# Two heads in one output block, half masks, and a new order in the first two attentions of a two-layer decoder

## The reference

```
# first attention: 16 heads of 8 features, causal
q = concat(rms_norm(q_c), q_r);  k = concat(rms_norm(k_c), k_r)
attn = softmax(q @ k.T * scale + triu(-inf));  x = x + (attn @ v) @ W_O.T

# local attention on ctx_1024: chunks of w = 64 positions, so C = 2 chunks;
# each query sees the previous, own and next chunk; a missing chunk gives zero keys and values
ck = stack(prev, own, next);  probs = softmax(q . k_e over 3 * w)
x = x + (probs . v_e) @ Wc

# relative attention of the second layer
score = ((q + u) @ k.T + shift((q + v) @ pos.T)) / sqrt(8)
x = x + softmax(score) @ val @ Wo + bo
```

## Time and profile before

| | us |
|---|---|
| median of 3 runs | 1391.49 (1387.20 to 1395.02) |
| the profiled execution | 1387.54, its span 1385.7 |
| busy: PE, DVE, ACT, POOL | 1139.1, 990.6, 835.2, 562.5 |
| mean granted clock of TensorE | 0.953 |

### The profile page before, as it was taken

How to read it: one execution, slowest core, us unless ns; L and a number is a source line. 1 busy time by engine, 2 the same in 40 slices (tenths; PEclk the granted TensorE clock), 3 DMA queues, 4 the chain that set the end, 5 groups by cost and what they waited for, 6 DMA issues and landing times. The chain is left out here.

```text
span 1385.7 us, 40959 instructions
## 1 busy us (share of the span) xinstructions
PE 1139.1 (82%) x12567; PEld 744.3 (54%) x12567; DVE 990.6 (71%) x3667; ACT 835.2 (60%) x1653; POOL 562.5 (41%) x750
## 2 busy tenths in 40 slices
PE   2788887887598888898589878888888758999998
PEld 1344444454355555555378456666666544665665
DVE  2588888885366666666466369999998739887885
ACT  1487878786277777777423378888887432342331
POOL 4777777772222222222010146666665911111120
PEclk9899999999599999999889999999999778999999
DMA  8000000000100000000022078888887540000000
GB/s 220 9 2 1 0 0 0 0 2 2 56 8 2 1 0 0 0 0 0 17 60 61 14 214 237 236 232 232 234 234 210 155 130 1 8 16 9 8 8 16
DMA packets 170484, 91.33 MB, mean 66 GB/s; under 512 B 8922, under 2 KB 168804, under 8 KB 170132
## 3 DMA queue, kind: packets, MB, share of 16 engines
q1 hardware_dynamic: 169860, 88.05, 23.3%
q0 software_dynamic: 528, 2.10, 0.5%
HBM read 52.11 MB, written 38.01 MB: 65 GB/s over the span
## 5 line engine op out<-in xcount | busy, mean ns | idle before, releaser
L821 POOL TENSOR_TENSOR rr<-ms_eps,minus_half 128x16 f32<-128x16 f32 x64 | 185.2, 2912 | 11.6 <-DVE ms_eps L1029 11.6
L550 PE MATMUL psum<-identb,stacks 128*128 128x128 bf16 x1800 | 138.3, 224 | 34.9 <-DVE stacks L1078 13.5
L1163 DVE TENSOR_REDUCE rowmax<-psum 128x4 f32<-128x768 f32 x128 | 123.1, 961 | 60.8 <-PE psum L2130 60.8
L550 PEld LDWEIGHTS psum<-identb,stacks 128*128 128x128 bf16 x1800 | 111.5, 100 | 65.7 <-issue 24.8
L1364 DVE CUSTOM_DVE_ANT_0 summed<-psum,pos_score 128x128 f32<-128x128 f32 x512 | 117.9, 285 | 23.5 <-PE psum L2330 19.9
L1930 ACT ACTIVATE pos_rows<-psum 128x512 f32<-128x512 f32 x72 | 43.0, 597 | 144.0 <-PE psum L2514 137.1
L2372 PE MATMUL psum<-consts,summed 128*128 128x128 f32 x512 | 84.4, 289 | 43.1 <-DVE summed L1370 41.7
L1068 DVE TENSOR_REDUCE rowmax<-psum 128x4 f32<-128x512 f32 x128 | 84.9, 686 | 34.6 <-PE psum L1996 34.6
L1816 ACT ACTIVATE probsT<-psum 128x512 f32<-128x512 f32 x128 | 76.9, 601 | 54.0 <-PE psum L641 39.8
L641 PE MATMUL psum<-probsT,values 128*32 128x128 f32 x2048 | 85.2, 282 | 26.1 <-DVE attn L667 21.7
L882 POOL TENSOR_TENSOR rest<-staged,stacks 128x128 f32<-128x128 f32 x32 | 13.7, 428 | 220.4 <-ACT stacks L533 220.4
(11 more groups left out here) (320 smaller groups left out, 3065.1 us busy)
## 6 DMA issues: line engine op xcount, KB each, us to landing
skew<-pos_rows SPq DMA_DIRECT2D x128, 258.0 KB, 3.8
pos_score<-skew SPq DMA_DIRECT2D x128, 256.0 KB, 4.0
X<-in_x_dram POOLq DMA_DIRECT2D x1, 2048.0 KB, 12.1
ctxT<-in_ctx_dram SPq DMA_DIRECT2D x1, 2048.0 KB, 10.6
yT<-in_ctx_dram SPq DMA_DIRECT2D x32, 64.0 KB, 1.8
ctxT<-in_ctx_dram SPq DMA_DIRECT2D x32, 64.0 KB, 1.8
out_dram<-X SPq DMA_DIRECT2D x8, 256.0 KB, 2.3
pos_rows<-in_ctx_dram SPq DMA_DIRECT2D x25, 64.0 KB, 1.9
```

What stands on the lines that cost most here:

```text
L550: last = pe.transpose(turned[:, t, :], stacks[:, which, 2 * t:2 * t + 2, :].rearrange("s h k -> s (h k)"), identb[:, :])
L821: pool.tensor_tensor(out=rr[:, par, i * H:(i + 1) * H], in0=ms_eps[:, i * H:(i + 1) * H], in1=minus_half[:, 0:H], op=ALU.pow).then_inc(A.r ...
L1163: dve.tensor_reduce(rowmax[:, par, PT * r:PT * r + PT].rearrange("s (h b) -> s b h", b=2), B.max_space, AX.X, ALU.max, negate=True).then_i ...
```

## The change

It has four parts.

- Output blocks: two heads share one block of 32 rows, the even group in rows 0 to 8, the odd one in rows 16 to 24; the odd group's products accumulate onto the even one's (whose weights are zero there). So `out_bank` is read over 256 columns, `outT` is half as wide, `turn_out` is two transposes and `normalise` one multiplication. Values are written to two places by parity (`value_slots`), and `v8` has a fourth slice.
- Half masks: a mask is four products of 256 columns, each over 64 of the 128 rows, alternating between the two halves of the rows and the two banks. Both banks wait for both maxima (or exponentials).
- Order in the first attention. DVE: `ln_stats` in front of the first `largest`, `query_parts` between the two. ACT: `save_xnT` between the two first parts; `save_again` (the copy of the turned stack with the maxima) behind `exps_turned` 2 and 3. PE: `scores` of the next batch ahead of `scores_turned`.
- Local attention: the two products of `sums` go; DVE adds the two chunks' keys (`key_sums`, from `k3T`), behind `normalise`; `save_kv` copies 128 columns and goes ahead of `save_q`; `key_top_1` and `turn_v` wait for the sums; `ln_stats` goes behind `largest` 2.

The diff, cut:

```diff
-        outT = sb("outT", [128, R, S])
+        outT = sb("outT", [128, R // 2, S])
+        by_pairs = values[:, :, :, :].rearrange("s a (m e) g -> s a m (e g)", e=2).rearrange("s a m (x w) -> s a m x w", w=HD)
+        SLOT_STEP = (GW + GW // 2) // HD
+        def value_slots(i):
+            return by_pairs[:, i, :, 0:SLOT_STEP + 1:SLOT_STEP, :]
...
+        def out_rows(q, r, p):
+            return q.out_bank[p * GW:(p + 1) * GW, (r // 2) * S:(r // 2 + 1) * S]
...
-                last = pe.matmul(q.out_bank[p * GW:(p + 1) * GW, r * S:(r + 1) * S], v, probsT[:, r % 2, p, :],
-                                 start=True, stop=True)
+                last = pe.matmul(out_rows(q, r, p), v, probsT[:, r % 2, p, :], start=(r % 2 == 0), stop=(r % 2 == 1),
+                                 skip_group_check=True)
...
-            act.activation(outT[:, :, :].rearrange("k r s -> k (r s)"), q.out_bank, ACT.Copy).then_inc(q.oT, 1)
+            act.activation(outT[:, :, :].rearrange("k r s -> k (r s)"), q.out_bank[:, 0:R // 2 * S], ACT.Copy).then_inc(q.oT, 1)
...
-            for r in range(R):
-                last = pe.transpose(q.out_bank[:, r * S:(r + 1) * S], outT[:, r, :], ident)
+            for j in range(R // 2):
+                last = pe.transpose(q.out_bank[:, j * S:(j + 1) * S], outT[:, j, :], ident)
...
-            if q.stacked:
-                for half in range(2):
-                    last = dve.tensor_tensor(
...
+            def mask_products(banks, turned):
+                for half in range(2):
+                    for k in range(2):
+                        rows = slice(k * STACK, (k + 1) * STACK)
+                        columns = banks[k].rearrange("s (p k) -> s p k", p=PT)[:, :, half * STACK:(half + 1) * STACK]
+                        pe.matmul(columns, mask_half[turned][rows, half, :], identb[rows, rows].unsqueeze(1).broadcast_to([STACK, PT, STACK]),
+                                  start=(half == 0), stop=False, skip_group_check=True)
             def masks(n, r):
-                for k in range(2):
-                    wait(pe, A.mx, n * R + r + k - 1)
-                    pe.matmul(A.max_bank[k], identb[:, :], causal4[:, :, :].rearrange("s p k -> s (p k)"),
-                              start=True, stop=False, skip_group_check=True)
+                wait(pe, A.mx, n * R + r)
+                mask_products(A.max_bank, 0)
...
+                if left >= 6:
+                    ln_stats(dve, A, b + 6, b + 6)
                 if left >= 2:
                     largest(b + 2, par, 0)
+                if left >= 3:
+                    query_parts(b + 3, 1 - par)
+                if left >= 2:
                     largest(b + 2, par, 1)
                 if left >= 3:
-                    query_parts(b + 3, 1 - par)
                     key_parts(b + 3)
-                if left >= 6:
-                    ln_stats(dve, A, b + 6, b + 6)
...
-                if left >= 1:
-                    save_again(b + 1, 1 - par)
                 if left >= 3:
                     top_query(b + 3, 1 - par)
-                    top_key(b + 3)
                 if left >= 5:
                     save_xnT(act, A, b + 5, xnT[:, :], A.proj, b + 5)
+                if left >= 3:
+                    top_key(b + 3)
                 exps_turned(b, 2)
                 exps_turned(b, 3)
+                if left >= 1:
+                    save_again(b + 1, 1 - par)
...
-                scores_turned(b, par, four, 2)
                 if left >= 2:
                     scores(b + 2, par, after_four, 0)
+                scores_turned(b, par, four, 2)
...
+                def key_sums(n, par):
+                    wait(dve, B.kv, 2 * n + 1)
+                    first, second = [k3T[:, par, c * 64:(c + 1) * 64].unsqueeze(1).broadcast_to([128, 2, 64]) for c in range(2)]
+                    dve.scalar_tensor_tensor(out=k3T[:, par, BOTH:2 * BOTH].rearrange("s (c k) -> s c k", c=2), in0=first,
+                                             scalar=one_rows[:, 0:1], in1=second, op0=ALU.subtract, op1=ALU.add).then_inc(B.kv, 1)
...
+                    if left >= 2:
+                        key_sums(b + 2, par)
+                    if left >= 1:
+                        largest(b + 1, 1 - par, 2)
                     if left >= 3:
                         ln_stats(dve, B, b + 3, b + 3)
-                    if left >= 1:
-                        largest(b + 1, 1 - par, 2)
...
                     if left >= 2:
+                        save_kv(b + 2, par)
                         save_q(b + 2, par)
-                        save_kv(b + 2, par)
...
-                    sums = B.ln_bank[:, 384:512].rearrange("s (c k) -> s c k", c=2)
-                    for c in range(2):
-                        last = pe.matmul(sums, both, ctxT[:, at(n), c * 64:(c + 1) * 64].broadcast_to([D, 2, 64]),
-                                         start=(c == 0), stop=(c == 1))
-                    last.then_inc(B.proj, 1)
```

More of the change, by code:

```diff
@@ L28 @@
 MAX_SLOT = 56
+MASKED = -1e30
 C_ID, C_CAUSAL, C_HEAD, C_REP, C_SIN = 0, 128, 256, 272, 400
@@ L221, in decoder @@
         projected = yT[:, 0:16, :].rearrange("s (a w) (h d) -> s a w h d", a=4, h=H)
-        causalT4 = yT[:, 16:18, :].rearrange("s a k -> s (a k)").bitcast(BF16).rearrange("s (p k) -> s p k", p=PT)
+        causalb = yT[:, 16:17, :].rearrange("s a k -> s (a k)").bitcast(BF16)[:, 0:S]
+        mask_blocks = causal4[:, :, :].rearrange("s (t h) (x w) -> s t (h x) w", t=2, w=S // 2)
+        mask_half = [causal4[:, 2 * turned:2 * turned + 2, :] for turned in range(2)]
         keysT = seqT[:, 0:16, :].rearrange("k a s -> k (a s)").bitcast(BF16).rearrange("k (a t s) -> k a t s", a=4, t=H // 2)
@@ L803, in _ @@
             pool.wait_ge(k0.ones, 1)
-            pool.memset(values[:, :, :, HD:HD + 1], 1.0).then_inc(k0.ones, 1)
+            for half in range(2):
+                ones_at = half * GW // 2 + HD
+                last = pool.memset(values[:, :, half:H:2, ones_at:ones_at + 1], 1.0)
+            last.then_inc(k0.ones, 1)
             pool.memset(minus_half[:, :], -0.5).then_inc(k0.half, 1)
@@ L808, in _ @@
             pool.wait_ge(k0.kvzero, 2)
-            pool.memset(v8[:, :, 0, HD:HD + 1], 1.0).then_inc(k0.kvzero, 1)
             for half in range(2):
+                ones_at = half * GW // 2 + HD
+                last = pool.memset(v8[:, :, half, ones_at:ones_at + 1], 1.0)
+            last.then_inc(k0.kvzero, 1)
+            for half in range(2):
+                ones_at = half * GW // 2 + HD
                 pool.wait_ge(k0.kvzero, 3 + half)
-                pool.memset(v8[half * STACK:(half + 1) * STACK, :, 1 + half, HD:HD + 1], 1.0).then_inc(k0.kvzero, 1)
+                pool.memset(v8[half * STACK:(half + 1) * STACK, :, 2 + half, ones_at:ones_at + 1], 1.0).then_inc(k0.kvzero, 1)
             pool.wait_ge(k0.kvzero, 5)
@@ L1002, in _ @@
             dve.tensor_copy(identb[:, :], ident).then_inc(k0.cast, 1)
-            dve.tensor_copy(causal4[:, :, :], consts[:, C_CAUSAL:C_CAUSAL + S].unsqueeze(1).broadcast_to([S, PT, S])).then_inc(k0.cast, 1)
+            dve.tensor_copy(causalb, consts[:, C_CAUSAL:C_CAUSAL + S]).then_inc(k0.cast, 1)
+            for turned in range(2):
+                dve.memset(mask_blocks[:, turned, 1 + turned, :], 0.0)
+                dve.memset(mask_blocks[:, turned, 2 - turned, :], MASKED)
             dve.wait_ge(k0.mask, 1)
-            dve.tensor_copy(causalT4[:, :, :], A.key_bank.bitcast(BF16)[:, 0:S].unsqueeze(1).broadcast_to([S, PT, S])).then_inc(k0.mask, 1)
+            for half in range(2):
+                rows = slice(half * STACK, (half + 1) * STACK)
+                keys_first = A.key_bank.bitcast(BF16)[rows, half * STACK:(half + 1) * STACK]
+                queries_first = consts[rows, C_CAUSAL + half * STACK:C_CAUSAL + (half + 1) * STACK]
+                for turned, triangle in enumerate([keys_first, queries_first]):
+                    last = dve.tensor_copy(mask_blocks[rows, turned, 0:4:3, :], triangle.unsqueeze(1).broadcast_to([STACK, 2, STACK]))
+            last.then_inc(k0.mask, 1)
             dve.tensor_scalar(qnws[:, :], qnw[:, :], SCALE, None, ALU.mult).then_inc(k0.qnws, 1)
@@ L1211, in cross_attention @@
                     ln_apply(dve, B, n, n)
+                    key_sums(n, n)
                     key_rest_of(n, n)
@@ L1687, in save_v @@
                     wait(act, B.o, (n - 3) * R)
-                    act.activation(v8[:, four, 0, 0:HD], B.ln_bank[:, USED:USED + HD], ACT.Copy)
+                    both = v8[:, four, 0:2, :].rearrange("s e g -> s (e g)").rearrange("s (x w) -> s x w", w=HD)[:, 0:SLOT_STEP + 1:SLOT_STEP, :]
+                    act.activation(both, B.ln_bank[:, USED:USED + HD].unsqueeze(1).broadcast_to([S, 2, HD]), ACT.Copy)
                     for half in range(2):
                         rows = slice(half * STACK, (half + 1) * STACK)
```

(5 more changed lines are left out.)

56 lines of the change are left out of this document (24 added, 32 removed).

## The result

The changed kernel takes 1339.76 us (median of 4 runs, 1338.67 to 1345.12), the kernel before, in runs beside it, 1390.43: a ratio of 0.964, 95% interval 0.960 to 0.968. The forecast was 1347, faster. The profiled execution is one of 1338.67, its span 1336.9 (before 1385.7).

What follows compares the result with a forecast made beforehand. Rings of waits bound the first and local attention, VectorE the relative one. Gains of 30+9+2+1.5=42.5 us from 1387.5 gave 1345, plus half of the 4 us to the run median: 1347; 8-in-10 range 1325 to 1368.

Steps and rivals of the forecast that it cites:

- DVE's own work: 8.15-0.07=8.08: First attention: with PE no longer waited for, a batch is VectorE's own work, 8.08 us, taken as 8.1 instead of 9.13.
- 1.74 instead of 1.96: First attention: upper end of the gain, 36 us, if the six operations on parts take 1.74 us instead of 1.96.
- First rival, a new wait there: First attention: waits among three nearly full engines make the batch 8.5 us, gain 18 instead of 30, total 1359; chance 0.2.
- The cover of 1.90 us: First attention: VectorE has 1.27 plus 0.63 = 1.90 us of work while TensorE does its piece, 0.43 to spare.
- PE's piece: First attention: TensorE's products from `turn_again` to the scores, forecast at 1.47 us after the change, 2.25 before including the semaphore.
- the ring itself: Local attention: waits over query copy, GpSimd's parts, `place_max`, `save_again`, `save_outT` and `project` set the 9.55 us batch; gain 0.3.
- it was about 0.2 us from being the later one: Local attention: the second path, exponential of the sums, value products, `turn_again`, caps the gain, about 0.2 us from being later.
- 9.55-0.29=9.26: Local attention: net 0.29 us less on the ring, from halved `save_outT`, no wait for `project`, less 0.17 for `save_kv` first.
- the local attention gains nothing: Rival: copying keys ahead of queries and the second path eat the local gain; 9 us less, 1356; chance 0.12.
- DVE, the bound, only `normalise`: Relative attention: VectorE, busy 260.8 of 292 us, is the bound; only `normalise` shortens, 32 times 0.07 = 2 us.
- The 1.5 us for the ends: Ends of the three attentions: `outT`, `turn_out` and `normalise` each save 0.21+0.25+0.07=0.53 us, 1.5 in all.
- The clock rival: First attention: an idler TensorE falls to half clock, its 6.6 us a batch becoming 11.1; kernel slower, up to 1435; chance 0.03.

## Why the prediction was right, and where it was not

**First attention: mechanism right, size too small.** The idle time in front of `largest` 0, the half masks side by side (0.45 against the 0.44 forecast for two groups) and DVE's own work as the new bound are there. The term that was mis-sized is "DVE's own work: 8.15-0.07=8.08". It measured 7.77. Of the 0.31, 0.33 is the query parts (1.18 to 0.85): 0.21 as GpSimd's addition no longer meets the conversion but a reduction from PSUM, which it doesn't stretch (0.68), and 0.12 as an independent reduction follows the third operation. Another 0.08 is a slip in the reckoning: the 8.15 counted `key_3` to its recorded end (231.28), but with work behind it the next operation starts 0.21 after its start, not 0.29. Against these stand 0.07 for the statistics (0.63 before, 0.70 now) and 0.03 for the key parts. The text had the faster parts as an end of its range ("1.74 instead of 1.96": they measured 0.85+0.89=1.74, and by the distance of starts they had taken 1.18+0.86=2.04 before) and did not take it. The runs with late parts and with the cut residual show both causes. Masks and statistics put back together cost 0.73 a batch and the parts 0.32, of the 1.36 that went (9.13 to 7.77); the new order of the scores and of ACT's copies and the halved output were not undone by themselves, so how the rest divides is open.

**First rival, a new wait there: not so.** The wait of the mask for two maxima costs PE 0.35 us and DVE nothing. The cover of 1.90 us was right (172.44 to 174.33: 1.89), while PE's piece is 1.60 (late statistics), not 1.47: 0.29 to spare, not 0.43. With full masks it is 2.02 (229.67 to 231.69, with both edits), where 1.90 was forecast.

**Local attention: the step that failed** is the ring itself, and with it "it was about 0.2 us from being the later one" (and even with 0.2 in hand, 0.3 a batch could not come). The text followed the batch over the query copy, `project` and GpSimd's parts to `place_max`, and saw the path over the exponential of the sums and the value products as the second. That second path already set the pace in the kernel before: there `turn_again` follows 0.15 behind the end of `place_max`, where 0.06 is enough if nothing else holds it (230.01 to 230.07), and it starts 0.35 behind the start of the value products, in both kernels. The ring that it closes had the same 9.05 us apart from `normalise` before and after. What the text priced did come true, on a path that does not bind: from `save_again` to the end of the next `place_max` it is 8.42 instead of 8.75, 0.33 less where 0.29 was forecast, and `turn_again` now follows that end by 0.42 instead of 0.15. With `turn_again` early the value products are out of the way and it follows `place_max` again; the batch then falls to 9.27 to 9.32, near the 9.55-0.29=9.26 of the text, but other waits bind there too, so that nearness proves nothing. What shortens only the earlier of two near equal paths gains nothing. The rival "the local attention gains nothing" was nearly the true case, though for one only of its two reasons, the second path: of the 2.3 us within the stage the batches explain 2.0 (31 times 0.063), and the run with two multiplications puts these down to `normalise`, 0.06 a batch, a term that the text had in the other two attentions and not in this ring. The other reason, the copy of the keys ahead of the queries, was not it: turning the two round changed nothing.

**Relative attention: the step "DVE, the bound, only `normalise`" failed, and the size is luck.** Its period fell by 0.009 (9.034 to 9.025), not by 0.07: in both kernels the next operation on DVE starts 0.38 or 0.48 behind the multiplication's start, in turn (0.48 at 937.42 to 937.90 before, 0.38 at 882.10 to 882.48 after), and later in the batch DVE idles as before (0.45, and 0.46 after), by its bracket for PE. "DVE, the bound" was read from a busy share of 89%; the batch was set elsewhere. The run with two multiplications there confirms that the merged one is worth nothing. Which wait sets this batch stays open. One candidate that the text did not weigh is the DMA traffic of this stage, 223 GB/s at a busy share of 0.83 before and 224 at 0.83 after (the earlier trace rows and above); no run separates it from a wait. Of the stage's 2.1 us the periods explain 0.3 (31 times 0.009). The others are within what the stage differs by from trace to trace.

**Stage ends and clock.** The 1.5 us for the ends can't be told apart from what else happens there: 1.8 went between the first two stages and 1.0 in the rest, 0.6 came between the second and third, and 2.2 went ahead of the first reciprocal, which the sum did not have at all. The clock rival did not come: granted clock 0.99 in the first attention with PE busy 192.97 of 235 us, and 1.00 from 65 us on. The row that this rival was priced by (1.04 us for eight turns) does not show a low clock, as the profile reports 1.00 for 28 to 33 us; but the same eight turns take 1.04 at 362.74 in the kernel before, where the granted clock is 0.50 (347.5 to 381 us), so the price stands. The rule of the Trainium skill that was weighed there ("TensorE: Matmul & The Clock Gate", section on a second HAM failure mode) speaks of a swing of the clock between groups of matmuls; the trace shows no such swing in this stage of the changed kernel. To the other rule of the Trainium skill, "VectorE: DVE Perf Modes", section on the TRN2 errata: in the first attention the merged multiplication and its follower stand 0.21 apart (171.05 to 171.26), the two before it took 0.27 (228.56 to 228.83), so 0.06 went, as on the ring of the local attention; by the page's cycles it would be an estimated 0.12. The measurement decides.

## What to carry to other kernels

Follow a ring of waits from bracket to bracket until it comes back to its start: what is not on it gains nothing. Before counting a gain on one, look up what else the point where paths meet (here `turn_again`) waits for in its engine's own order: if two end within 0.1 us of each other, shorten both or expect nothing. Once an engine becomes the bound, price its work by the distance of starts without idle time, and look for the operations that are longer than their like: a 0.50 beside a 0.29 is a collision that a new order may remove, or bring. Read the bound of a stage from what a batch waits for, not from an 89% busy share.

## What the runs showed of the hardware

A GpSimd addition of two 128 x 128 operands in SBUF (0.45 us) stretched the DVE operation on SBUF that it met. In the kernel before that was the conversion in the query parts, in all 24 steady batches (0.43 to 0.60 us, median 0.50, where the conversion in the key parts takes 0.29); with the parts late it was mostly the third operation (median 0.53 instead of 0.29). A DVE reduction from PSUM beside it kept its 0.68, in 23 of 24 batches of the changed kernel; cut to one column the addition stretched nothing. The Trainium skill, "VectorE: DVE Perf Modes", section on two Vector instructions with no wait between them, says that VectorE's second SBUF read interface, which the second of two SBUF inputs is read through (or the input of an operation in a two-port mode), is shared with GpSimd; the trace agrees as to which operations were stretched, and gives the size (in which mode the conversion ran no row shows; its 256 elements take the 0.29 us of a two-input operation on 128). A DVE operation on 128 elements that waits for the one before it on a semaphore starts 0.31 to 0.33 behind it, an independent one 0.21. In three runs the granted clock fell to 0.50 (the lower of its two levels) once within the first attention: in the two with late statistics, where that batch was 0.9 and 1.3 us longer than its like, and in the one with late parts (0.2). The busy time of the kernel with late statistics alone ahead of it and in it, columns as in the earlier trace rows:

```profile
187.00:195.50 8.50, 6.52 (x109) 4.36 (x109) 7.19 (x25) 7.29 (x15) 6.86 (x6) 1.00 0.00 0
195.50:204.50 9.00, 7.77 (x109) 5.30 (x109) 7.26 (x26) 6.23 (x14) 6.62 (x5) 0.81 0.00 0
```

The same 109 products kept PE busy for 6.52 us ahead of the dip and 7.77 in it. Each of the three falls came at a turn of the loop, at which PE idles 1.3 to 1.6 us in these kernels and 1.0 in the changed one; but the other turns of the loop had the same idle time and no fall, so why the clock fell stays open.
